# Two attention blocks and two feed-forward blocks on one core: the seam between the first attention and the ternary feed-forward is rewritten

## The reference, cut to what matters

```python
x = x + _L0_xattn_ref(_layernorm(x), ctx, Wq, Wkv, Wout, bout)
x = x + _L0_ffn_ref(_layernorm(x), w_gate, w_up, w_down)
# attention: out = softmax(q k^T) v per head, then Wout out + bout
# _layernorm(x) = (x - mean) / sqrt(var + 1e-5), per row
# feed-forward: act_quant per token (absmax to 8 bits), gate and up products with
# ternary weights, silu(gate) * up, Walsh-Hadamard transform, act_quant, down product
```

## Time and profile before

| | us |
|---|---|
| median of three runs | 2478.67 |
| the three runs | 2474.19, 2480.57, 2478.67 |
| span of the profiled execution, first to last instruction | 2477.6 |
| TensorE busy | 2036.3 (82%) |
| VectorE, ScalarE, GpSimd busy | 1527.1, 1251.3, 1311.8 |

### The profile page before, as it was taken

How to read it: one execution, slowest core, us unless ns; L and a number is a source line. 1 busy time by engine, 2 the same in 40 slices (tenths; PEclk the granted TensorE clock), 3 DMA queues, 4 the chain that set the end, 5 groups by cost and what they waited for, 6 DMA issues and landing times. The chain is left out here.

```text
span 2477.6 us, 35421 instructions
## 1 busy us (share of the span) xinstructions
PE 2036.3 (82%) x11666; PEld 771.7 (31%) x11666; DVE 1527.1 (62%) x2377; ACT 1251.3 (51%) x1832; POOL 1311.8 (53%) x852
## 2 busy tenths in 40 slices
PE   3999999999999946999848998999974207999970
PEld 1222222222222222444322222222213204665540
DVE  5555555555555356776557777777735745777757
ACT  3666665677776444554324666666654004544520
POOL 1666676666667615676232232222213566888860
PEclk8999999999999978999977999999985558999995
DMA  2122221222221172000022222332302006777648
GB/s 99 39 75 59 72 70 41 66 66 74 61 71 31 28 228 70 1 1 1 1 47 56 54 52 56 58 62 60 58 13 74 1 2 207 224 223 222 204 144 340
DMA packets 176984, 204.97 MB, mean 83 GB/s; under 512 B 52503, under 2 KB 124695, under 8 KB 174657
## 3 DMA queue, kind: packets, MB, share of 16 engines
q1 hardware_dynamic: 153712, 163.97, 24.1%
q0 software_dynamic: 17408, 33.67, 4.2%
q10 hardware_dynamic: 5712, 5.45, 0.7%
HBM read 159.55 MB, written 59.93 MB: 89 GB/s over the span
## 5 line engine op out<-in xcount | busy, mean ns | idle before, releaser
L657 DVE TENSOR_REDUCE a_negmax<-a_ps_max 128x2 f32<-128x1024 f32 x256 | 312.1, 1219 | 226.9 <-PE a_ps_max L467 226.9
L1087 DVE TENSOR_REDUCE a_negmax<-a_ps_max 128x1 f32<-128x512 f32 x512 | 331.8, 682 | 112.1 <-PE a_ps_max L933 109.9
L1034 ACT ACTIVATE a_probs<-a_ps_st 128x512 f32<-128x512 f32 x512 | 286.5, 595 | 170.3 <-PE a_ps_st L954 169.0
L591 ACT ACTIVATE a_probs<-a_ps_st 128x1024 f32<-128x1024 f32 x256 | 262.0, 1024 | 208.8 <-PE a_ps_st L487 208.8
L427 POOL TENSOR_TENSOR a_added_up<-a_added_up,a_probs 128x1024 f32<-128x1024 f32 x128 | 301.2, 2353 | 29.7 <-ACT a_probs L591 27.4
L498 PE MATMUL a_ps_o<-a_probs,a_values 128*64 128x512 f32 x1024 | 276.2, 618 | 0.0
L427 POOL TENSOR_TENSOR a_added_up<-a_probs 128x1024 f32<-128x1024 f32 x64 | 150.3, 2349 | 228.6 <-ACT a_probs L591 228.6
L933 PE MATMUL a_ps_max<-a_k_st,a_q_st 96*128 96x512 f16 x512 | 204.7, 400 | 34.7 <-DVE a_negmax L1087 15.0
L954 PE MATMUL a_ps_st<-a_q_st,a_k_st 97*128 97x512 f16 x512 | 198.5, 390 | 15.3 <-ACT a_probs L1034 11.5
L43 PE MATMUL s_gu<-s_xT,s_gu_h 128*128 128x384 f16 x768 | 188.9, 328 | 1.9 <-DVE s_xT L2211 1.9
L888 POOL TENSOR_TENSOR a_heads_out<-a_plain,a_inverse 128x512 f32<-128x512 f32 x32 | 40.8, 1274 | 243.9 <-DMA a_inverse<-a_dram_inverse 243.9
(11 more groups left out here) (416 smaller groups left out, 4343.8 us busy)
## 6 DMA issues: line engine op xcount, KB each, us to landing
s_raw<-in_guT SPq DMA_DIRECT2D x32, 768.0 KB
a_inverse<-a_dram_inverse SPq DMA_DIRECT2D x128, 128.0 KB, 2.9
m_y_tok<-f_nothing SPq DMA_DIRECT2D x16, 1024.0 KB, 10.2
c_yg<-m_y_tok SPq DMA_DIRECT2D x16, 1024.0 KB, 8.3
a_ctx_in<-in_ctx SPq DMA_DIRECT2D x32, 256.0 KB, 3.1
a_w_raw<-in_wgT SPq DMA_DIRECT2D x32, 256.0 KB, 3.0
a_w_raw<-in_wuT SPq DMA_DIRECT2D x32, 256.0 KB, 3.0
a_w_raw<-in_wdT SPq DMA_DIRECT2D x32, 256.0 KB, 2.8
```

The source lines that it names most:

```text
L591: act.activation(probs[:, s % RING, :, :], ps_st[:, :, :], ACT.Exp).then_inc(exped, 1)
L657: dve.tensor_reduce(negmax[:, v % 2, :, i % KD], ps_max[:, :, :], AX.X, ALU.max, negate=True).then_inc(maxed, 1)
L1034: act.activation(probs[:, s // HG % 3, s % HG, :], ps_st[:, s % 2, :], ACT.Exp, scale=DH1 ** -0.5).then_inc(exped, 1)
L1087: dve.tensor_reduce(negmax[:, g % 2, at:at + 1], ps_max[:, i % 2, :], AX.X, ALU.max, negate=True).then_inc(maxed, 1)
```

## The change

The scales block skips the aggregation of the first 15 batches (argument `first`), which is now done at the end of the first attention. There, the last group doesn't go through DRAM: for tile 62 (in step 253) and for tile 63 (behind the loop) TensorE sums with a matrix of ones into 64 rows per head of `ps_max`, VectorE inverts the whole [128, 512] tile out of PSUM and multiplies the tile by it. ScalarE ends the attention with a square root that nothing reads. The float32 and bfloat16 identities are made once, in the first attention. In the feed-forward only the Hadamard constants are loaded, GpSimd casts them after the fourth quantised tile, and VectorE instead of ScalarE normalises the first four tiles, from the mean and scale directly.

```diff
-def layer_norm_scales(nc, tag, stats, mv, rstd):
+def layer_norm_scales(nc, tag, stats, mv, rstd, first=0):
-            for b in range(B):
+            for b in range(first, B):
                 dve.bn_aggr(mv[:, b, :], stats[:, b, :]).then_inc(step, 1)
...
+    LAST = KD * B - 2
...  (first_attention, SyncE)
-            compact_sums(GROUPS - 1)
-            spread_inverse(GROUPS - 1)
...  (GpSimd)
-            for v in range(KD * B - KD, KD * B):
+            for v in range(KD * B - KD, LAST):
                 normalise(v)
...  (TensorE)
+            def sum_last(v):
+                pe.wait_ge(added, 3 * v + 3)
+                pe.wait_ge(maxed, T)
+                for half, rows in enumerate(HALVES):
+                    last = nc.tensor.matmul(ps_max[rows, v % 2, :], ones[:, 0:DH0], added_up[:, v % UPS, half, :], start=True, stop=True)
+                last.then_inc(summed, 1)
             def project_out(n, k):
-                pe.wait_ge(normalised, KD * n + k + 1)
+                if KD * n + k < LAST:
+                    pe.wait_ge(normalised, KD * n + k + 1)
+                else:
+                    pe.wait_ge(last_normalised, KD * n + k - LAST + 1)
...
+                if s == T - 3:
+                    sum_last(LAST)
             weigh_values(T - 1)
-            sum_up(GROUPS - 1)
+            sum_last(LAST + 1)
...  (ScalarE)
             take_out(KD * B - 1)
-            keep_sums(GROUPS - 1)
+            act.wait_ge(kept, KD * B)
+            act.activation(magic[:, 0:1], magic[:, 0:1], ACT.Sqrt)
...  (VectorE)
+            def normalise_last(v):
+                inv = (xn, ctx_in)[v - LAST]
+                dve.wait_ge(summed, GROUPS + v - LAST)
+                dve.reciprocal(inv[:, :], ps_max[:, v % 2, :]).then_inc(last_inverted, 1)
+                dve.wait_ge(last_inverted, v - LAST + 1)
+                dve.wait_ge(kept, v + 1)
+                place = heads_out[:, v // KD % 2, v % KD, :]
+                dve.tensor_tensor(place, place, inv[:, :], ALU.mult).then_inc(last_normalised, 1)
...
             norm(0)
+            dve.tensor_copy(ident[:, :], ident32[:, :])
...
+            for n in range(B - 2):
+                dve.bn_aggr(mv[:, n, :], stats[:, n, :])
+            normalise_last(LAST)
             add_residual(B - 2)
-            invert(GROUPS - 1)
+            normalise_last(LAST + 1)
+            dve.wait_ge(stats_in, B - 1)
+            dve.bn_aggr(mv[:, B - 2, :], stats[:, B - 2, :])
             add_residual(B - 1)
...  (ternary_ffn, SyncE)
-            sp.dma_start(ident32[:, :], d["ident"]).then_inc(const_in, 16)
...  (GpSimd)
-            pool.wait_ge(const_in, 32)
+            pool.wait_ge(const_in, 16)
+            pool.wait_ge(xq_ready, G)
             pool.tensor_copy(had..., hb...)
...  (TensorE and ScalarE)
-            wait_ge(const_set, 4)
-            wait_ge(const_in, 32)
+            wait_ge(const_set, 3)
-            normalise(0)
-            normalise(1)
             for k in range(G):
                 quantise_tokens(k)
-                if k + 2 < G:
-                    normalise(k + 2)
...  (VectorE)
+            def normalise(k):
+                need(dve, xq_ready, k - 1)
+                dve.tensor_scalar(xn[:, k % 2, :], x_all[:, k, :], mv[:, k, 0:1], rstd[:, k, :], ALU.subtract, ALU.mult).then_inc(normed, 1)
-            dve.wait_ge(const_in, 32)
-            dve.tensor_copy(ident[:, :], ident32[:, :]).then_inc(const_set, 1)
+            normalise(0)
+            normalise(1)
+            measure_tokens(0)
+            measure_tokens(1)
             dve.tensor_scalar(gmean...)
             dve.scalar_tensor_tensor(shift...).then_inc(shifted, 1)
             dve.wait_ge(shifted, 1)
-            measure_tokens(0)
-            measure_tokens(1)
             for k in range(G):
+                if k + 2 < G:
+                    normalise(k + 2)
+                    measure_tokens(k + 2)
                 keep_tokens(k)
-                if k + 2 < G:
-                    measure_tokens(k + 2)
```

More of the change, by code:

```diff
@@ L58, in _ @@
         def _(dve):
-            for b in range(B):
+            for b in range(first, B):
                 dve.bn_aggr(mv[:, b, :], stats[:, b, :]).then_inc(step, 1)
-            dve.wait_ge(step, B)
+            dve.wait_ge(step, B - first)
             dve.tensor_scalar(veps[:, :], mv[:, :, 1], LN_EPS, None, ALU.add).then_inc(step, 1)
@@ L65, in _ @@
             dve.reciprocal(rstd[:, :], root[:, :]).then_inc(step, 1)
-            dve.wait_ge(step, B + 2)
+            dve.wait_ge(step, B + 2 - first)
             dve.tensor_tensor(t[:, :], rstd[:, :], rstd[:, :], ALU.mult).then_inc(step, 1)
-            dve.wait_ge(step, B + 3)
+            dve.wait_ge(step, B + 3 - first)
             dve.tensor_tensor(t[:, :], t[:, :], veps[:, :], ALU.mult).then_inc(step, 1)
-            dve.wait_ge(step, B + 4)
+            dve.wait_ge(step, B + 4 - first)
             dve.tensor_scalar(t[:, :], t[:, :], -0.5, 1.5, ALU.mult, ALU.add).then_inc(step, 1)
-            dve.wait_ge(step, B + 5)
+            dve.wait_ge(step, B + 5 - first)
             dve.tensor_tensor(rstd[:, :], rstd[:, :], t[:, :], ALU.mult).then_inc(step, 1)
@@ L76, in _ @@
         def _(act):
-            act.wait_ge(step, B + 1)
+            act.wait_ge(step, B + 1 - first)
             act.activation(root[:, :], veps[:, :], ACT.Sqrt).then_inc(rooted, 1)
@@ L243, in over_batches, with first_attention @@
         turn((B - 2 + q, q))
-def first_attention(nc, x_all, stats, mv, rstd, wq, means, d):
+def first_attention(nc, x_all, stats, mv, rstd, wq, means, ident, ident32, d):
     STEPS = 16
@@ L274, in first_attention @@
         bout = sb("bout", [P, 1], F32)
-        ident32 = sb("ident32", [P, P], F32)
         shift = sb("shift", [P, P], F16)
@@ L307, in first_attention @@
         w_in = [sem(f"w_in{q}") for q in range(SLOTS)]
+        last_inverted, last_normalised, stats_in = sem("last_inverted"), sem("last_normalised"), sem("stats_in")
         w_used, w_rounded, w_step, w_total = (sem(n) for n in ("w_used", "w_rounded", "w_step", "w_total"))
@@ L404, in _ @@
                 sp.wait_ge(w_in[q], 16 * 2 * CHUNKS // SLOTS)
-            sp.wait_ge(inverse_in, 16 * HG * GROUPS)
+            sp.wait_ge(inverse_in, 16 * HG * (GROUPS - 1))
         @block.gpsimd
@@ L672, in add_residual @@
                 dve.wait_ge(residual, n + 1)
-                dve.bn_stats(stats[:, n, :], xb)
+                dve.bn_stats(stats[:, n, :], xb).then_inc(stats_in, 1)
             def weight_sums():
@@ L1142, in rotary_attention, with ternary_ffn @@
     clear(nc, semaphores)
-def ternary_ffn(nc, x_all, stats, mv, rstd, wq, means, ident, d, y_tok):
+def ternary_ffn(nc, x_all, stats, mv, rstd, wq, means, ident, ident32, d, y_tok):
     G = 4
@@ L1237, in _ @@
                 sp.dma_start(lower.rearrange("(p k) (c n) -> p (k c) n", k=SEL, n=P), nothing[:, :].unsqueeze(1).to_broadcast([P, SEL * KD, P])).then_inc(lower_cleared, 16)
-            sp.wait_ge(const_in, 32)
+            sp.wait_ge(const_in, 16)
             sp.wait_ge(lower_cleared, 16 * B)
@@ L1339, in down @@
                     last.then_inc(y_done, 1)
-            pe.wait_ge(const_set, 4)
-            pe.wait_ge(const_in, 32)
+            pe.wait_ge(const_set, 3)
             for k in range(G):
@@ L1408, in keep_half @@
                 act.activation(qT[:, NC_ // 2 * half:NC_ // 2 * half + NC_ // 2, :], ps_qT[:, :, :], ACT.Copy).then_inc(qT_kept, 1)
-            act.wait_ge(const_set, 4)
-            act.wait_ge(const_in, 32)
-            normalise(0)
-            normalise(1)
+            act.wait_ge(const_set, 3)
             for k in range(G):
                 quantise_tokens(k)
-                if k + 2 < G:
-                    normalise(k + 2)
             for n in SLOTS:
@@ L2489, in build @@
         ident = sb("ident", [P, P], BF16)
+        ident32 = sb("ident32", [P, P], F32)
         y_tok = nc.dram_tensor("m_y_tok", (2 * SEL * B * P, D), F32, kind="Internal").ap()
@@ L2492, in build @@
         with nc.sbuf_tensor("wq", [P, 3, KD * FF], BF16) as wq, nc.sbuf_tensor("means", [P, 3], F32) as means:
-            first_attention(nc, x_all, stats, mv, rstd3, wq, means, d)
-            layer_norm_scales(nc, "ln1_", stats, mv, rstd)
-            ternary_ffn(nc, x_all, stats, mv, rstd3, wq, means, ident, d, y_tok)
+            first_attention(nc, x_all, stats, mv, rstd3, wq, means, ident, ident32, d)
+            layer_norm_scales(nc, "ln1_", stats, mv, rstd, B - 1)
+            ternary_ffn(nc, x_all, stats, mv, rstd3, wq, means, ident, ident32, d, y_tok)
         rotary_attention(nc, x_all, stats, mv, rstd3, d)
```

## The result

The changed kernel takes 2456.64 us (median of 4 runs, 2454.1 to 2461.02) against 2479.62 for the kernel before in the same comparison (4 runs, 2474.19 to 2481.84): ratio 0.9916, 95% interval 0.9888 to 0.9944. Two later comparisons of the same two kernels give 0.992 (0.9892 to 0.9949) and 0.9912 (0.9887 to 0.9936).

A forecast was written before the change was run, and what follows sets the result against it. Waits at the attention's end (DRAM round trip) and feed-forward's start (identity DMA, ScalarE chain) bound the seam. 9.9 + 1.0 + 9.1 = 20.0; 2477.6 - 20.0 + 1.1 = 2458.7 us; own range 2454 to 2464, ends 2453 and 2468.

The forecast's parts named there:

- Wide reciprocal 3.1, between 0.69 and 7.8: Attention's end: VectorE's [128, 512] inversion takes 3.1 us by slope from two widths; bounds 0.69 and 7.8.
- Piece 3 warm, 1.12: Attention's end: without the idle hole, TensorE's last projection piece takes 1.12 us at full clock, half of 2.26.
- Tail 9.9: Attention's end: last statistics end at 867.5 instead of 877.38, gain 9.9 us; bounds 5.2 to 10.4.
- The room for tile 62: Attention's end: 14 aggregations (1.0) and tile 62's reciprocal fit where VectorE waits 11.35 us before the residual.
- Block 1.0: Scales block: skipped aggregations and the table load done earlier gain 1.0 us; 0.1 if loaded again, 1.2 at most.
- Entry 9.1: Feed-forward's start: first gate product 12.75 us after its first instruction instead of 21.82, gain 9.1; bounds 7 to 9.9.
- The clock's rise, worth 1 either way: Feed-forward's start: TensorE's rise to full clock, today at 907.2, could move by 2 either way, worth 1 us.
- The cast's new wait costs nothing: Feed-forward's start: GpSimd's cast waits for the fourth tile; its reader comes 5.3 us after the gate product, so covered.
- A: Rival: only one end pays, something hidden holds the feed-forward's start; 12 us gain left, 2466.7; chance 0.08.
- B: Rival: wide reciprocal takes 7.8, attention's end gains 3.7, time 2464.9, chance 0.07; in "B +" sums, the feed-forward's first instruction.
- C: Rival: feed-forward's loop slower with TensorE at half clock, 1.7 us a slot; after 16 slots near 2486; chance 0.02.
- D: Rival: table loaded again (0.9 us, 2459.6, within the forecast) or a wait orders the same chain; no separate chance.

The follow-up runs named there:

- e7: The changed kernel with one more wide reciprocal on VectorE ahead of tile 62's; 2461.75 us, one run.
- e3: The kernel before with only the attention's last two sums changed (`sum_last`, `normalise_last`); 2464.56 us against 2476.61, ratio 0.9953.
- e5: The changed kernel without the unread square root at the attention's end; 2466.82 us, one run.
- e2: The changed kernel run again with no edit; 2455.32 us.
- e6: The changed kernel with GpSimd casting the Hadamard constants once landed, not after the fourth quantised tile; 2465.99 us, one run.
- e4: The kernel before with only the feed-forward's start changed: identities kept, VectorE normalising four tiles, Hadamard cast behind the fourth; 2465.79 us, ratio 0.9968.
- e12: The changed kernel run again with no edit, beside another kernel on the same chip; 2454.61 us.

## Why the prediction was right

- *What bounds the seam*: right. Both holes were waits for work that could be elsewhere, and with all engines meeting on either side the 20.0 arrive at the feed-forward's end (20.2).
- *`sum_last(62)` costs 1.02*: 4.05 - 3.03 = 1.02.
- *Wide reciprocal 3.1, between 0.69 and 7.8*: 3.36. The slope from 1 and 16 columns (5.3) was low by 1 ns a column. The Trainium skill's repeat count of 8 ("VectorE: DVE Perf Modes", section "First, the fixed hardware budget"), taken as 8 cycles a column, gave an estimate of 4.3; the measured 3.36 decides, and that reading was too much.
- *Piece 3 warm, 1.12*: 1.12, at a granted clock of 1.00. Before, TensorE had stood still for 9.74 us ahead of this stretch, and the clock was at 0.50 in it (872 to 876).
- *Tail 9.9*: 9.4 to 9.7. The reciprocal's 0.26 is the difference from 9.9 to 9.7; from there to 9.4 it is the DMA round trip of the kernel before, which repeats to 0.3 only. Tile 62 waited for GpSimd and was in time, as stated; e7 shows how much room it had.
- *The room for tile 62*: enough, but read from the wrong row. The prediction gives the 11.35 us of idle time before the last residual. The 14 aggregations and tile 62's reciprocal lie before the residual of batch 14, and there VectorE waited 5.81. About 4.8 of work (1.0, 3.1 and 0.69) had to go in, so the room was smaller than written. The row in the kernel before:

```profile
857.33 0.75 DVE L671 SCALAR_TENSOR_TENSOR x_all<-a_ps_misc,a_bout,x_all 128x512 f32<-128x512 f32 x1 [5.81 <-PE a_ps_misc L513]
```

- *Block 1.0*: 1.23. The hand-over into the block is 0.25 shorter (1.00 for 1.25), which I hadn't counted, and it comes with the tail (e3). That the load would be exposed is shown by e5.
- *Entry 9.1*: 9.2 to 9.4. First reduction at B + 0.96 (forecast 1.04), gate product at B + 12.64 in e2 (forecast 12.75), shift 0.17, `keep_tokens` beside the cast 0.42, all as written.
- *The clock's rise, worth 1 either way*: nothing. From the kept scales to the last statistics the feed-forward takes 360.2 to 360.7 in the kernel after, 360.4 and 360.5 before.
- *The cast's new wait costs nothing*: right, but my reason for it was too narrow. The prediction counted what the early cast cost the shift (1.8) and no more; by e6 the wait also keeps a normalisation free, worth 0.95.
- *Sum 20.0*: 20.0 in the traces at the kept scales, 20.1 by the seams. That it is this close is partly luck: the tail gave 0.2 to 0.5 less than forecast, block and entry 0.2 and 0.1 to 0.3 more. The medians of three comparisons give 23.0, 21.3 and 22.2; their intervals hold 20. Whether the missing 1 to 3 are scatter or a small gain in the later stages is open: across all traces here the second attention lies between 591 and 601 and the experts between 553 and 569, and no experiment separates so little.
- *The ends of the range*: the high end, 2468, doesn't follow from its terms. A leaves 12 of the 20.0, B takes 6.2 more, and with 3 for the scatter that is 2475.9. The low end is 2454.2 by its terms, not 2453. Neither bears on the outcome.
- *Rivals*: A falls with e4, whose entry gives its 9.1 alone. D falls with the kernel after, which has no table load at L78; e5 shows that it would have stood there. B's 7.8 falls with the row of 3.36. C falls with the clock at full from 887 on, 16 after the block's first instruction (25.5 before).

## What to carry to other kernels

Between two points where all engines meet, add up the chain from rows: here each part came within 0.5 us, and the sum of 20 within 0.1, partly because the errors cancelled. Where the stages around it scatter by several us, compare the stretch and not only the whole, and profile the unchanged kernel twice before explaining a difference in it. When a small VectorE instruction is placed in a free gap, look at what GpSimd does in that gap: one multiplication of 14 columns took 1.2 us there instead of 0.17.

## What the runs showed of the hardware that was not expected

- A VectorE normalisation with a single SBUF tensor input (float32, 512 columns) stands still behind a GpSimd cast: 1.49 for 0.54 (e6). The copy of a tile from PSUM beside the same cast does not (0.42), nor does a maximum over 512 columns in SBUF inside another GpSimd instruction (0.69).
- A VectorE reciprocal costs 6.25 ns a column from PSUM (1.76 us for 256, 3.36 for 512).
- One program, with a seam that repeats to 0.01 us, has stages of some 600 and 555 us that differ by 6 and 7 us from execution to execution (after, e2, e12). The cause is open.
